# A hybrid attention and mixture-of-experts kernel: nine hidden chunks instead of six before the first expert weights, and a new order of the side steps

## The chip, the cores and the metric

The kernel runs on one core of a Trainium2 chip. The metric is the device time of one execution in microseconds (us). TensorE (PE in the profile) multiplies into eight PSUM banks, VectorE (DVE), ScalarE (ACT) and GpSimd (POOL) do the element work, and SyncE (SP) issues all DMA transfers. Each engine runs its own instructions strictly in the order of the program, and a wait on a semaphore holds up everything behind it on that engine.

## The reference

Four sequences ("rows") of 1024 tokens with 128 features each go through four residual blocks:

```python
x = x + attn_a(layernorm(x))   # no softmax: per-token 8x8 kv sums over heads, rms norms, gelu MLP
x = x + ffn(layernorm(x))      # 32 experts of width 64; the top 8 weigh, all 32 are computed
x = x + attn_b(layernorm(x))   # causal softmax attention, 16 heads, window of 64
x = x + ffn(layernorm(x))
# ffn: for each expert  acc += (u * silu(g)) @ dw.T * w_e[:, None]
```

## The kernel before, in words

**Chunks.** A row is two groups of 512 tokens, and each group goes through the ffn twice, so a row has four ffn stages `f` = 0 to 3 and the kernel 16 of them. A stage is 16 chunks; a chunk is two experts (128 hidden values) by 512 tokens. For each chunk PE makes the gate and the up product (`gate_up`, three matmuls each, since the operands are split into a high and a low part), ACT applies silu from PSUM into a buffer `work` (`silu`), DVE multiplies the up product in (`gated`), POOL multiplies the experts' combination weights in (`hidden`), and PE multiplies by the down weights (`down`, two instructions in the trace), which adds into one bank. In the stream `down` follows `gate_up` by three chunks. The gate and up banks hold three chunks, `work` holds six.

**Combination weights.** A stage's weights are made by the steps `route`, `r_sum`, `top`, `weigh`, `comb`, `cnorm` and `weighT`. The last one copies them into `combT` on ACT; SP sends that to DRAM (L649) and reads it back spread over the partitions in four quarters of four chunks, the first as eight transfers (L661), the others as two each (L666). The spread buffer holds two quarters; a later quarter waits until POOL is done with the one before in its place.

**Side steps.** Everything else (norms, the first attention, MLP, projections) is cut into named steps. `PLAN` is a table written out by hand or by a search: for each stage, which steps stand behind which chunk ("slot"). `own`, `ahead` and `back` say whether the step is of this row, the next or the one before. Each engine runs through the table and executes its own half of each step, so a step moved in the table moves on every engine that takes part. During the softmax attention, which has stages of its own (`attn`, three slots for each tile of 128 tokens), the same table is used. `x_stats` is the start of a norm on DVE and waits for the row's input transfer `x_buf<-x` (L631); `m_stats`, `m_rstd` (POOL), `m_apply` (ACT), `moe_turn` (PE), `z_hi` (ACT), `z_lo` (DVE) are the norm ahead of an ffn stage; `h_sq1` to `h_sum` are the rms norms of the first attention; `attend` (POOL), `kvsum`, `wterm`, `wred` (DVE) are its sums for one tile; `seq_turn`, `keys`, `queries`, `values` prepare the softmax attention.

**The lead.** Before the first stage no weights are there. `AHEAD` is the order of the steps until then. In it `early n` is PE's `gate_up` of chunk n and `lead n` is ACT's `silu` and DVE's `gated` of that chunk; `FIRST` says how many chunks stand there. `elu_first`, `qkv_first`, `qkv_next`, `expo` and `qscale` are the steps of the first attention on ACT and PE, `w_hi` and `w_lo` split the expert weights, `masks` are constants on POOL.

Of the kernel before, what the change touches and what calls it, by code (L numbers as in the profile page):

```python
# [80 lines left out]
def back(*steps):  # L81
# [3 lines left out]
FIRST = 6  # L85
# [15 lines left out]
        15: ahead(("qkv", 5)),
    },
    (0, "third"): {
        0: ahead(("wred", 3), ("h_sq1", 0), ("h_red1", 0), ("h_g2", 0), ("h_newton1", 0), ("qkv", 6), ("h_sq2", 0)),
        1: ahead(("h_red2", 0), ("qkv", 7), ("h_pow2", 0), ("h_newton2", 0)),
        3: own(("y_back", 0), ("s_stats", 0)) + ahead(("h_scale", 0), ("h_gain", 0), ("h_sum", 0)) +
            own(("s_rstd", 0)),
        4: ahead(("expo", 1), ("elu", 1)),
        5: ahead(("qscale", 1)),
        6: ahead(("attnT", 0), ("attend", 4), ("x_add", 0)),  # L110
        7: ahead(("mlp1", 0)),
        8: ahead(("attend", 5)) + own(("s_apply", 0)) + ahead(("mlp2", 0)),
        10: own(("bias", 0)) + ahead(("kvsum", 4)) + own(("seq_turn", 0)),
        11: ahead(("wterm", 4)) + own(("keys", 0)) + ahead(("m_stats", 0), ("m_rstd", 0)),
        12: own(("queries", 0)),
        14: ahead(("m_apply", 0)) + own(("values", 0)) + ahead(("kvsum", 5)),
        15: ahead(("moe_turn", 0), ("attend", 6)),
# [1559 lines left out]
```

## Time and profile before

| what | us |
|---|---|
| median of 3 runs | 970.69 |
| lowest and highest run | 967.74, 975.84 |
| the profiled execution's own time | 970.32 |
| its span from first to last instruction | 968.5 |

The times below are counted from the start of the span; 1.8 us of the execution lie outside it. The busy shares are means over stages that are bound by different things, so each stage is read for itself.

### The profile page before, as it was taken

How to read it: one execution, taken by the hardware profiler on the slowest of the kernel's cores; microseconds unless marked ns; L12 is line 12 of the kernel's file. 1: busy time of each engine (PE TensorE's matmuls, PEld its weight loads, DVE VectorE, ACT ScalarE, POOL GpSimd, SP SyncE). 2: the span in 40 equal slices, each digit the busy share in tenths (PEclk: the TensorE clock that was granted, in tenths of full speed). 3: DMA queues.
4: the chain of work that ended last, by engine and by line, in shares of the span. 5: the costliest groups of instructions: out<-in, count | busy, mean ns of one | idle time of the engine just before them, and what ended most of it. 6: DMA issues, size and time to landing. Idle time of an engine off the chain costs nothing.

```text
span 968.5 us, 16816 instructions
## 1 busy us (share of the span) xinstructions
PE 895.2 (92%) x5456; PEld 623.2 (64%) x5456; DVE 653.0 (67%) x1471; ACT 611.6 (63%) x1876; POOL 663.8 (69%) x617
## 2 busy tenths in 40 slices
PE   2467999898999999999999999999999999999998
PEld 1145666685667666687666666687666667667665
DVE  5898876897768748698648756798635348447522
ACT  4446676993665576795775585896556377486531
POOL 6786888675687759576669768666666545646654
PEclk8559999999899999999999999999999999999999
DMA  6006254016343626240433534340344530713352
GB/s 193 0 1 142 52 128 89 2 46 136 64 123 76 139 60 157 58 121 13 98 92 87 146 83 108 74 129 17 87 106 102 135 68 27 159 38 102 88 133 65
DMA packets 64903, 85.75 MB, mean 89 GB/s; under 512 B 5232, under 2 KB 30768, under 8 KB 64560
## 3 DMA queue, kind: packets, MB, share of 16 engines
q1 hardware_dynamic: 64816, 84.68, 36.4%
q8 instruction: 43, 0.70, 0.3%
q14 instruction: 44, 0.36, 0.1%
HBM read 79.39 MB, written 5.28 MB: 87 GB/s over the span
## 4 chain that ended last, share of the span: by engine, by line
PE 69%; DVE 10%; ACT 7%; POOL 5%; issue 4%; DMA 3%; SPq 1%; DVEq 0%; ACTq 0%; POOLq 0%
PE bank L1542 19%; PE bank L1519 11%; PE bank L1521 10%; PE bank L1520 10%; ACT probs L1081 4%; PE bank L1578 4%; PE bank L1563 3%; PE bank L1592 2%; POOL work L872 2%; DVE probsT L1346 2%; PE bank L1406 1%; DMA spread_w<-comb_dram 1%; DVE w_terms L1188 1%; PE bank L1556 1%; DMA x_buf<-x 1%
## 5 line engine op out<-in xcount | busy, mean ns | idle before, releaser
L872 POOL TENSOR_TENSOR work<-work,spread_w 128x512 f32<-128x512 f32 x256 | 333.8, 1318 | 171.0 <-DVE work L1304 151.7
L1304 DVE TENSOR_TENSOR work<-work,bank 128x512 f32<-128x512 f32 x256 | 172.1, 683 | 185.3 <-PE bank L1521 93.1
L1542 PE MATMUL bank<-work,down_w 128*128 128x512 f32 x512 | 262.7, 598 | 1.9 <-POOL work L872 1.9
L1056 ACT ACTIVATE work<-bank 128x512 f32<-128x512 f32 x256 | 150.3, 596 | 176.5 <-PE bank L1521 171.9
L1519 PE MATMUL bank<-z_hi,gate_hi 128*128 128x512 f32 x256 | 168.0, 656 | 4.9 <-ACT work L1056 2.7
L1081 ACT ACTIVATE probs<-bank,neg_max 128x96 f32<-128x96 f32 x512 | 166.3, 386 | 5.5 <-DVE neg_max L1332 3.9
L880 POOL TENSOR_TENSOR probs<-probs,prob_inv 128x768 f32<-128x768 f32 x64 | 95.1, 1486 | 59.9 <-DVE prob_inv L1340 59.6
L1081 ACT ACTIVATION_READ_ACCUMULATOR probs<-bank,neg_max 128x1 f32 x512 | 127.6, 252 | 0.0
L1542 PEld LDWEIGHTS bank<-work,down_w 128*128 128x128 f32 x512 | 95.3, 189 | 29.6 <-POOL work L872 5.6
L1519 PE MATMUL bank<-z_hi,up_hi 128*128 128x512 f32 x256 | 101.8, 397 | 3.1 <-DVE work L1304 3.1
L1521 PE MATMUL bank<-z_hi,gate_lo 128*128 128x512 f32 x256 | 102.0, 398 | 0.0
L1521 PE MATMUL bank<-z_hi,up_lo 128*128 128x512 f32 x256 | 101.5, 397 | 0.0
L1520 PE MATMUL bank<-z_lo,gate_hi 128*128 128x512 f32 x256 | 101.2, 395 | 0.0
L1520 PE MATMUL bank<-z_lo,up_hi 128*128 128x512 f32 x256 | 100.4, 392 | 0.0
L829 POOL TENSOR_TENSOR kv_terms<-elu,qkv 128x1024 f32<-128x1024 f32 x32 | 81.8, 2562 | 12.5 <-DVE elu L1153 7.2
L1346 DVE COPY probsT<-bank 96x512 f32<-96x512 f32 x128 | 80.2, 666 | 3.6 <-PE bank L1578 3.2
L1332 DVE TENSOR_REDUCE neg_max<-bank 128x4 f32<-128x384 f32 x128 | 64.8, 547 | 20.1 <-PE bank L1563 19.2
L1519 PEld LDWEIGHTS bank<-z_hi,gate_hi 128*128 128x128 f32 x256 | 49.0, 191 | 42.4 <-issue 31.0
L1578 PE MATMUL bank<-ident,probs 128*96 128x128 f32 x512 | 69.8, 278 | 6.8 <-DVE probsT L1346 6.0
L1520 PEld LDWEIGHTS bank<-z_lo,gate_hi 128*128 128x128 f32 x256 | 49.3, 193 | 33.7 <-issue 30.6
L1563 PE MATMUL bank<-keysT,qm 32*128 32x96 f32 x1024 | 69.2, 269 | 0.0
L1563 PEld LDWEIGHTS bank<-keysT,qm 32*128 32x128 f32 x1024 | 66.4, 188 | 0.0
(155 smaller groups left out, 1467.2 us busy)
## 6 DMA issues: line engine op xcount, KB each, us to landing
spread_w<-comb_dram SPq DMA_DIRECT2D x96, 512.0 KB, 6.7
spread_w<-comb_dram SPq DMA_DIRECT2D x128, 128.0 KB, 3.0
vals<-v_dram SPq DMA_DIRECT2D x16, 384.0 KB, 4.0
x_buf<-x SPq DMA_DIRECT2D x8, 256.0 KB, 4.3
v_dram<-v_tok SPq DMA_DIRECT2D x8, 256.0 KB, 6.8
out<-xs SPq DMA_DIRECT2D x8, 256.0 KB, 3.1
spread_w<-wg SPq DMA_DIRECT2D x1, 1024.0 KB, 7.1
spread_w<-wu SPq DMA_DIRECT2D x1, 1024.0 KB, 9.2
```

The costliest lines, as they stand in the source:

```text
L872: pool.tensor_tensor(work[:, n % WORK], work[:, n % WORK], spread_w[:, n // EACH % 2, s % EACH], ALU.mult).then_inc(hid_gated, 1)
L880: pool.tensor_tensor(pr, pr, prob_inv[:, i % 2, part].unsqueeze(2).broadcast_to([P, HALF_BLOCKS, KW]), ALU.mult).then_inc(probs_normed, 1)
L1056: act.activation(work[:, n % WORK], bank[GATE_BANKS[ring_of(row, f, s)]], ACT.Silu).then_inc(silu_ready, 1)
L1081: a = act.activation(probs[:, i % 2, m], bank[hg][:, b * KW:(b + 1) * KW], ACT.Exp, bias=neg_max[:, i % 2, m:m + 1], accum_out=prob_sum[:, ...
L1304: dve.tensor_tensor(work[:, n % WORK], work[:, n % WORK], bank[UP_BANKS[ring_of(row, f, s)]], ALU.mult).then_inc(gated_ready, 1)
L1346: dve.tensor_copy(probsT[:, b], bank[4 + b % 2][0:KW, :]).then_inc(probsT_copied, 1)
L1519: pe.matmul(dst, w_hi[:, cols], h, start=True, stop=False)
L1520: pe.matmul(dst, w_hi[:, cols], l, start=False, stop=False)
L1521: pe.matmul(dst, w_lo[:, cols], h, start=False, stop=True).then_inc(ready, 1)
L1542: pe.matmul(bank[Y_BANK], down_w[:, c], work[:, n % WORK], start=(c == 0), stop=(c == CH - 1)).then_inc(down_done, 1)
L1563: mm = pe.matmul(bank[hg][:, KW * b:KW * (b + 1)], qm[feats, i // T, NB * (i % T) + b].rearrange("p j q -> p (j q)"), keysT[feats, first:f ...
L1578: mm = pe.transpose(bank[4 + b % 2][0:KW, P * hg:P * (hg + 1)], probs[:, i % 2, hg * NB + b], ident[:])
```

## The change

`FIRST` becomes 9. Chunks 6 to 8 of the first stage have no room in `work`, so they go into `probs`, the buffer of the softmax probabilities, which is not in use yet; `work_of` says where a chunk lies, and `work_before` which chunk has to be through its `down` product before a buffer is written again. Both tables, `PLAN` and `AHEAD`, are replaced as a whole: the same steps in another order.

```diff
-FIRST = 6
+FIRST = 9
...
     (0, "first"): {
...
-        9: ahead(("x_stats", 1), ("x_rstd", 1)) + own(("m_apply", 1)),
-        10: own(("moe_turn", 1)) + ahead(("attend", 2), ("attend", 3)) + own(("z_hi", 1), ("z_lo", 1)),
+        9: own(("m_apply", 1)) + ahead(("kvsum", 1), ("wterm", 1)) + own(("moe_turn", 1), ("z_hi", 1)) +
+            ahead(("attend", 2)) + own(("z_lo", 1)) + ahead(("x_apply", 1)),
...
     (0, "attn"): {
...
-        25: ahead(("weighT", 0)),
+        19: ahead(("weighT", 0)),
...
     (1, "third"): {
-        0: ahead(("wterm", 3)),
...
+        1: own(("seq_turn", 0)) + ahead(("wterm", 3)) + own(("values", 0)),
...
+        def work_of(n):
+
+            if WORK <= n < FIRST:
+                return probs[:].rearrange("p r m k -> p r (m k)")[:, (n - WORK) // 3, GT * ((n - WORK) % 3):GT * ((n - WORK) % 3 + 1)]
+            return work[:, (n if n < WORK else n - FIRST) % WORK]
+
+        def work_before(n):
+            return n - (FIRST if n < FIRST + WORK else WORK) if n >= FIRST else -1
...
-                wait(act, down_done, n - WORK + 1)
-                act.activation(work[:, n % WORK], bank[GATE_BANKS[ring_of(row, f, s)]], ACT.Silu).then_inc(silu_ready, 1)
+                wait(act, down_done, work_before(n) + 1)
+                act.activation(work_of(n), bank[GATE_BANKS[ring_of(row, f, s)]], ACT.Silu).then_inc(silu_ready, 1)
...
-                pe.matmul(bank[Y_BANK], down_w[:, c], work[:, n % WORK], start=(c == 0),
+                pe.matmul(bank[Y_BANK], down_w[:, c], work_of(n), start=(c == 0),
```

Three places show what the tables do. The first is ACT at the end of the lead. `scratch<-attn` is `h_sq1`, `qkv<-bank` and the `elu<-bank` behind it are `qkv_next` 3, `elu<-elu 128x1024` is `expo`, `combT<-bank` is `weighT`, the writes of `work` are `lead`, and the two `elu<-elu 128x4x16x4` are `qscale`. Before:

```order
L984 ACTIVATE scratch<-attn 128x512
L964 ACTIVATE qkv<-bank 128x384
L965 ACTIVATE elu<-bank 128x256
L972 ACTIVATE elu<-elu 128x1024
L1025 ACTIVATE combT<-bank 32x512
L1056 ACT_TABLE_LOAD
L1056 ACTIVATE work<-bank 128x512 x2
```

Here is the same place on ACT after the change (eight lines further down in the file).

```order
L992 ACTIVATE scratch<-attn 128x512
L972 ACTIVATE qkv<-bank 128x384
L973 ACTIVATE elu<-bank 128x256
L980 ACTIVATE elu<-elu 128x1024
L1064 ACT_TABLE_LOAD
L1064 ACTIVATE work<-bank 128x512 x2
L986 ACTIVATE elu<-elu 128x4x16x4
L987 ACTIVATE elu<-elu,lam_coef 128x4x16x4
L1033 ACTIVATE combT<-bank 32x512
L1064 ACTIVATE work<-bank 128x512 x4
```

A table load, two `silu` and the two instructions of `qscale` now stand ahead of the copy that releases the weights.

The second place is POOL from the last side step of the lead through the first `hidden` products (`work<-work,spread_w`). `tok_rms` is the end of `h_pow2`, `x_buf<-x_buf,attn` is `x_add`, and `var_eps` to `shift` are a `rstd` step. Before:

```order
L872 TENSOR_TENSOR work<-work,spread_w 128x512 x3
L844 TENSOR_SCALAR tok_ms<-tok_ms 128x4
L845 TENSOR_TENSOR tok_rms<-tok_ms,minus_half 128x4
L872 TENSOR_TENSOR work<-work,spread_w 128x512 x2
L850 TENSOR_TENSOR x_buf<-x_buf,attn 128x512
L872 TENSOR_TENSOR work<-work,spread_w 128x512 x3
L815 TENSOR_SCALAR var_eps<-moments 128x4
```

The same stretch of POOL after the change:

```order
L852 TENSOR_SCALAR tok_ms<-tok_ms 128x4
L853 TENSOR_TENSOR tok_rms<-tok_ms,minus_half 128x4
L880 TENSOR_TENSOR work<-work,spread_w 128x512 x3
L858 TENSOR_TENSOR x_buf<-x_buf,attn 128x512
L880 TENSOR_TENSOR work<-work,spread_w 128x512 x3
L880 TENSOR_TENSOR probs<-probs,spread_w 128x512
L823 TENSOR_SCALAR var_eps<-moments 128x4
```

`x_add` moved from behind chunk 4 to behind chunk 2, `h_pow2` ahead of chunk 0, and `m_rstd` from behind chunk 7 to behind chunk 6.

The third place is DVE in the first ffn stage of row 1, `(1, "first")`: `w_terms` and `attn<-w_terms` are `wterm` 7 and `wred` 7, `xs<-x_buf,bank` is `proj`, `stats<-x_buf` is `x_stats` of row 2, and each `work<-work,bank` is `gated` of one chunk. Before:

```order
L1304 TENSOR_TENSOR work<-work,bank 128x512
L1188 TENSOR_TENSOR w_terms<-elu,kv 128x1024
L1194 TENSOR_REDUCE attn<-w_terms 128x128
L1139 BN_STATS stats<-x_buf 128x6 x4
L1142 BN_AGGR moments<-stats 128x2 x4
L1304 TENSOR_TENSOR work<-work,bank 128x512 x3
```

The same stage on DVE after the change:

```order
L1202 TENSOR_REDUCE attn<-w_terms 128x128
L1254 TENSOR_TENSOR xs<-x_buf,bank 128x512
L1312 TENSOR_TENSOR work<-work,bank 128x512 x2
L1266 TENSOR_TENSOR z_lo<-bank,z_hi 128x512
L1147 BN_STATS stats<-x_buf 128x6 x4
L1150 BN_AGGR moments<-stats 128x2 x4
L1207 TENSOR_REDUCE head_ms<-scratch 128x64
```

`x_stats` moved from behind chunk 3 to behind chunk 5, and `z_lo` stands ahead of it now.

## Rows read from the trace of the kernel before

**Rows 1.** The page, parts 1 and 2: busy time, and the granted clock in 40 slices.
```profile
PE 895.2 (92%) x5456; PEld 623.2 (64%) x5456; DVE 653.0 (67%) x1471; ACT 611.6 (63%) x1876; POOL 663.8 (69%) x617
...
PEclk8559999999899999999999999999999999999999
```

**Rows 2.** Busy time by stretch: length, then each engine, granted clock, DMA share, GB/s.
```profile
13.90:72.46 58.56, 28.05 (x66) 14.82 (x65) 54.13 (x95) 27.16 (x67) 45.85 (x38) 0.56 0.08 26
...
94.15:129.22 35.07, 33.19 (x133) 22.41 (x134) 27.88 (x66) 21.36 (x46) 28.69 (x25) 1.00 0.39 94
...
230.19:280.48 50.29, 46.74 (x170) 31.35 (x171) 34.12 (x71) 30.36 (x57) 33.22 (x28) 0.93 0.50 114
...
396.17:457.02 60.85, 57.83 (x728) 44.83 (x727) 48.60 (x106) 50.05 (x268) 40.15 (x40) 1.00 0.23 60
```

**Rows 3.** Timeline of ACT, end of the lead: start, length, what, idle time before.
```profile
72.49 0.63 ACT L984 ACTIVATE scratch<-attn 128x512 f32<-128x512 f32 x1 [1.45 <-DVE attn L1194]
...
73.81 1.06 ACT L972 ACTIVATE elu<-elu 128x1024 f32<-128x1024 f32 x1
75.95 0.59 ACT L1025 ACTIVATE combT<-bank 32x512 f32<-32x512 f32 x1 [1.09 <-PE bank L1461]
76.64 1.28 ACT L1056 ACT_TABLE_LOAD   x1
77.94 1.09 ACT L1056 ACTIVATE work<-bank 128x512 f32<-128x512 f32 x2
...
79.43 0.42 ACT L978 ACTIVATE elu<-elu 128x256 f32<-128x256 f32 x1
79.74 0.50 ACT L979 ACTIVATE elu<-elu,lam_coef 128x256 f32<-128x256 f32 x1
```

**Rows 4.** Timeline of SP and of POOL around the first quarters of weights.
```profile
76.56 0.35 SPq L649 DMA_DIRECT2D comb_dram<-combT  x1
...
92.81 1.29 POOL L872 TENSOR_TENSOR work<-work,spread_w 128x512 f32<-128x512 f32 x1 [4.53 <-DMA spread_w<-comb_dram]
...
99.14 1.15 POOL L815 TENSOR_SCALAR var_eps<-moments 128x4 f32<-128x4 f32 x1
...
101.97 2.50 POOL L872 TENSOR_TENSOR work<-work,spread_w 128x512 f32<-128x512 f32 x2
```

**Rows 5.** Timeline of PE behind the first weights.
```profile
94.15 1.12 PE L1542 MATMUL bank<-work,down_w 128*128 128x512 f32 x2 [0.35 <-POOL work L872]
95.11 1.05 PE L1440 MATMUL bank<-w_w,attnT 128*128 128x128 f32 x8
...
101.65 0.40 PE L1521 MATMUL bank<-z_hi,up_lo 128*128 128x512 f32 x1
101.89 1.02 PE L1542 MATMUL bank<-work,down_w 128*128 128x512 f32 x2
103.75 0.66 PE L1400 MATMUL bank<-ident,z 128*128 128x128 f32 x4 [0.83 <-ACT z L931]
```

**Rows 6.** Timelines of SP, DVE and PE, first ffn stage of row 1; a stretch of 3 us.
```profile
231.54 1.20 SPq L631 DMA_DIRECT2D x_buf<-x  x2
...
234.60 1.22 DVE L1194 TENSOR_REDUCE attn<-w_terms 128x128 f32<-128x1024 f32 x1
240.33 0.87 DVE L1139 BATCH_NORM_STATS2 stats<-x_buf 128x6 f32<-128x128 f32 x4 [4.50 <-DMA x_buf<-x]
...
242.24 0.50 PE L1519 MATMUL bank<-z_hi,up_hi 128*128 128x512 f32 x1 [3.07 <-DVE work L1304]
...
246.00:249.00 3.00, 3.00 (x11) 2.61 (x12) 1.52 (x3) 0.24 (x1) 2.67 (x6) 0.50 0.00 0
```

**Rows 7.** Timeline of DVE in the lead: the same operation twice.
```profile
49.04 3.26 DVE L1188 TENSOR_TENSOR w_terms<-elu,kv 128x1024 f32<-128x1024 f32 x1
...
56.90 1.22 DVE L1188 TENSOR_TENSOR w_terms<-elu,kv 128x1024 f32<-128x1024 f32 x1
```

**Rows 8.** Who waited for whom, from 125 us on: total, times, longest.
```profile
PE bank L1480 <- DVEq L1249: 0.9, 1, 0.9
```

More of the change, by code:

```diff
@@ L111 @@
[L111 to L117, printed above, removed]
+        0: ahead(("qkv", 6)),
+        1: ahead(("qkv", 7)),
@@ L173 @@
[L173 to L181 removed]
+        0: ahead(("wterm", 2), ("wred", 2), ("kvsum", 3)) + own(("weighT", 1)),
@@ new lines @@
+        6: own(("s_apply", 1)) + ahead(("attend", 6), ("moe_turn", 0), ("z_hi", 0)),
+        7: ahead(("z_lo", 0), ("route", 0), ("r_sum", 0), ("top", 0)),
+        8: ahead(("weigh", 0), ("comb", 0), ("kvsum", 5)) + own(("seq_turn", 1)),
+        9: ahead(("wterm", 5), ("wred", 5), ("kvsum", 6)) + own(("keys", 1)),
+        11: ahead(("attend", 7)) + own(("queries", 1), ("bias", 1)) + ahead(("wterm", 6), ("wred", 6)),
+        13: ahead(("kvsum", 7)) + own(("values", 1)) + ahead(("wterm", 7), ("cnorm", 0)),
@@ new lines @@
+        6: ahead(("x_apply", 0)),
+        7: back(("route", 2), ("r_sum", 2)) + own(("h_gain", 1)),
+        8: back(("top", 2)),
+        9: back(("weigh", 2)) + ahead(("x_turn", 0)),
+        10: ahead(("qkv", 0)) + back(("comb", 2)),
+        11: own(("h_sum", 1), ("attnT", 1)) + back(("cnorm", 2)) + ahead(("qkv", 1)) + own(("x_add", 1)),
+        12: back(("weighT", 2)),
+        13: own(("mlp1", 1)) + ahead(("qkv", 2)),
+        14: own(("mlp2", 1)),
+        15: own(("m_stats", 1), ("m_rstd", 1)) + ahead(("qkv", 3)),
@@ new lines @@
+    (2, "fourth"): {
+        0: own(("queries", 0)),
+        3: ahead(("mlp2", 0), ("m_stats", 0), ("m_rstd", 0)),
+        4: own(("y_back", 1), ("s_stats", 1), ("s_rstd", 1)),
+        5: ahead(("wterm", 4), ("wred", 4), ("kvsum", 5), ("m_apply", 0)),
+        6: ahead(("moe_turn", 0), ("z_hi", 0), ("z_lo", 0)) + own(("s_apply", 1)) + ahead(("wterm", 5)),
+        8: ahead(("route", 0)),
+        9: ahead(("r_sum", 0), ("top", 0), ("wred", 5), ("attend", 6), ("weigh", 0), ("comb", 0)),
+        10: own(("values", 0)) + ahead(("cnorm", 0), ("kvsum", 6)),
+        11: own(("seq_turn", 1)),
+        12: ahead(("wterm", 6)) + own(("keys", 1)),
+        13: own(("queries", 1)),
+        14: own(("values", 1)) + ahead(("wred", 6)),
+    },
@@ L291 @@
-    (3, "second"): {
-        0: own(("mlp1", 1)),
-        1: own(("mlp2", 1), ("m_stats", 1)),
-        2: own(("m_rstd", 1)),
-        5: own(("m_apply", 1)),
-        6: own(("moe_turn", 1), ("z_hi", 1), ("z_lo", 1)),
-        7: own(("route", 1), ("r_sum", 1), ("top", 1)),
-        9: own(("weigh", 1), ("comb", 1), ("cnorm", 1), ("y_back", 0), ("s_stats", 0), ("s_rstd", 0)),
-        10: back(("m_stats", 3), ("m_rstd", 3)),
-        12: own(("s_apply", 0), ("weighT", 1)),
-        14: own(("bias", 0)) + back(("m_apply", 3)),
-        15: own(("seq_turn", 0)),
-    },
```

414 lines of the change are left out of this document (200 added, 214 removed).

## The prediction

> **What bounds the kernel now.** The page comes first: PE is busy for 92% of the span, the next engine for 69% [rows 1], so the most that any new order can win is PE's idle time, 73 us, plus what the lower clock costs. The slices of the granted clock say where that lies: 8, 5, 5, 5 at the start, an 8 behind 190 us, a 9 behind 240, and 9s after that [rows 1]. The table by stretch then parts the kernel in three.
>
> The lead is DVE's. From 13.90 us to 72.46 DVE is busy for 54.13 us of 58.56 and PE for 28.05, at a mean clock of 0.56 [rows 2]. Time that PE loses there counts only through the moment at which the first weights come. That chain is read in the timelines: DVE's last sum ends at 72.46, ACT makes `h_sq1`, `qkv_next` 3 and `expo`, copies the weights out at 75.95 and SP sends them at 76.56 [rows 3, 4]. The second quarter lands in time for `hidden` of chunk 4 at 92.81, for which POOL waited 4.53 us [rows 4], and PE's `down` of it starts at 94.15 [rows 5]: 17.6 us after the send. From there to the first `down` of the next stage at 129.22 PE is busy for 33.19 of 35.07 us [rows 2].
>
> The first ffn stage of row 1 has a wait that can be named. DVE finishes the last first-attention sum at 235.82 and stands for 4.50 us, until 240.33, in `x_stats` of row 2: its two transfers `x_buf<-x` were issued at 231.54 only [rows 6]. `gated` of the next chunks is queued behind it on DVE, so PE stands for 3.07 us, and a stretch behind it runs at clock 0.50 though PE is never idle in it [rows 6]. 0.50 is the 1.2 GHz level, 1.00 is 2.4 GHz. The stage takes 50.29 us with 46.74 of PE and a mean clock of 0.93 [rows 2].
>
> Elsewhere PE is close to full: a softmax stage of 60.85 us has 57.83 of PE [rows 2], and the longest wait of the same kind as a bunched norm behind 125 us is 0.9 us [rows 8]. A new order there can give little and may take some.
>
> **The change, part by part.**
>
> *Ahead of the first weights.* On DVE the same steps stand before the last sum, with `x_stats` of the second group moved into an idle place before 13.90 us. It holds four `BN_STATS`, 0.87 us [rows 6], and its closing aggregate; I estimate 1.25 for both, so the last sum ends at 71.2. Bounds: if the rest of DVE's idle time went too, 58.56 - 54.13 = 4.4 us [rows 2], it would end at 66.8. If one `w_terms` met a POOL instruction more than before, 3.26 - 1.22 = 2.0 us [rows 7], it would end at 74.5 with none of the gain. I take 71.2, since the order on DVE hardly changes.
>
> Behind that sum ACT now has more to do. Before, from 72.49 to the copy's end at 76.54, ACT made three steps and waited 1.09 us for PE [rows 3]. Now it is `h_sq1` and `qkv_next` 3 (73.81 - 72.49 = 1.32), `expo` 1.06, the table load with the gap around it (77.94 - 76.54 = 1.40), two `silu` in 1.09, `qscale` in two instructions (79.43 to 80.24, 0.81) and the copy in 0.59 [rows 3]. Together 6.3 us, since `h_sq1` is the first of them and waits for the last sum: from 71.2 to 77.5, where the copy ends, one microsecond later than before.
>
> So `hidden` of chunk 4 comes 16.25 us after the send, as it did, at about 93.8, and `down` of it at 95.1. PE then has less to do before the next stage: one group of gate and up products stands earlier (six starts 0.24 apart, 1.40 us) and so does `mlp2` (under 1.05) [rows 5], 31.0 us in place of 33.19. But `m_rstd` stands behind `hidden` of 4, 5 and 6 on POOL. These take 1.25 each (2.50 for two), `m_rstd` 2.83 (99.14 to 101.97), and `m_apply` with PE's start another 1.78 (101.97 to 103.75) [rows 4, 5]. So `moe_turn` can start at 93.8 + 3.7 + 2.8 + 1.8 = 102.1, while PE has three `down` of 0.96 and one group of 1.40 until then and is through at 99.4. It idles for 2.7 us. The stage's end: 95.1 + 31.0 + 2.7 + 0.3 of the idle time that the stage had besides, and half a microsecond for `probs` as a new buffer, is 129.6, against 129.22: **+0.4**.
>
> The nine chunks let PE finish its early products sooner and wait longer before the weights come. Where PE waited like that the clock fell to 0.50 (the 3.00 us stretch in [rows 6]). One such spell, taken as twice that stretch and a little, 6.8 us at half rate, costs 3.4 us. It may come or not, so I take half, **+1.7**. Bounds of the lead in all: -3 with an early last sum and no spell, +7 with a late one and a spell. Sum: **+2.1**.
>
> *The Trainium skill on this.* ACT's switch of tables shows 1.28 us of load, and 1.40 from the end of the copy to the first `silu` [rows 3]. The Trainium skill, page "ScalarE: Activation LUTs", section "What ACT_TABLE_LOAD costs", adds a drain of 1.38 us to a load of 1.28. By it the copy would come 1.3 us later still, and the whole 968.2; the trace shows no room for such a drain.
>
> *The wait of row 1's first stage.* `weighT` of row 1 moves from slot 25 to slot 19 of the softmax stage of row 0, two tiles earlier. A stage of eight tiles takes 60.85 us where I have it as a row [rows 2], so two tiles are some 15 us, in the quicker stages nearer 11. SP sends the input of row 2 behind the quarters of these weights, so it is issued earlier by about as much, at 220 to 222. On top of that `x_stats` moves two slots later, about 4.5 us. A transfer issued at 231.54 was there at 240.33; one issued ten microseconds earlier is there at 230, well ahead of a reader at 240. The wait goes. What it cost: 50.29 - 46.74 = 3.55 us of PE idle and 0.07 x 50.29 = 3.5 us of clock [rows 2], together 7.0. The four `BN_STATS` still stand ahead of a `gated`, and `z_lo` now with them, so something of the idle time stays: **-6.5**, between -7 and -4 (the 4 is the 4.50 us wait without its clock).
>
> *Side steps put together.* In several places steps that had slots between them now share one: `seq_turn` and `values` of the softmax attention, `z_lo` with `route`, and `weigh`, `comb` and `cnorm` in slot 12 of the second stages. Each engine does the same work, but PE must wait for a copy on another engine inside a slot. The nearest row is PE waiting 0.9 us for DVE, the longest of its pair behind 125 us [rows 8]. I price one such wait net of what the other moves give back: **+1.0**, from 0 to +5 (five places at 0.9).
>
> *Softmax stages.* They have 3.02 us of PE idle in 60.85 [rows 2]; the moves put fewer norm steps into some and more into others. **0**, within 3 us either way, what one stage has.
>
> **How the numbers follow.** The profiled execution took 970.32 us, 1.8 of them outside the span, and the median of three is 970.69; I start from the first. 970.32 + 2.1 - 6.5 + 1.0 + 0 = 966.9, so **967** us, 0.4% faster. A measurement of this kernel can hardly tell less than 1%, 9.7 us, from no change.
>
> **Rivals.**
>
> *Faster by over 1%.* The rest of DVE's 4.4 us of idle time in the lead goes as well, and the last sum ends at 66.8. The copy ends 6.3 us later, at 73.1, 3.4 us earlier than before. The stage behind it gives another 0.6 (the terms above: +0.4 with a copy 1.0 later), the early products keep the clock at 1.00, and nothing is lost by the side steps: 970.3 - 3.4 - 0.6 - 6.5 = 959.8. For it speaks that DVE alone bounds the lead; against it, that ACT has two `silu`, a table load and `qscale` more ahead of the copy, and that little moves on DVE there. Chance 0.25.
>
> *Slower than before.* In the lead the same `w_terms` takes 1.22 us in one place and 3.26 in another [rows 7]; I take it that a POOL instruction beside it is the cause. If the new order lets three more of them meet one before the last sum, it comes 6.1 us later, and the clock's 3.4 us are due in full: 970.3 + 6.1 + 0.4 + 3.4 - 6.5 + 1.0 = 974.7. It decides from 1.7 us of such clashes on (6.5 - 1.0 - 3.4 - 0.4). Against it: nearly all sums of the lead stand where they stood. Chance 0.12. The Trainium skill, page "SBUF — State Buffer", section "SBUF: two separate sides", has the port pair that these two engines share as an exclusive lock, held for a whole instruction; by that rule each meeting costs up to the other's length, and the two lengths in [rows 7] agree with it.
>
> *The gain doesn't come, or comes back.* If the transfer still lands late, or the new slot makes DVE late for `gated` in the same way, 6.5 shrinks to 1: 972. For it: four steps stand behind `x_stats` in the slot now. Against it: the ten microseconds of lead. Chance 0.13.
>
> The forecast itself has 0.50. The range is **955 to 977**: the lower end is the faster rival with 3 us more from the softmax stages and something from the side steps, the upper the slower rival with half the side steps' bound on top. Faster by over 1%, below 961: 0.18 of the faster rival's 0.25, and 0.12 from the forecast with two of its terms at their lower bounds, **0.30**. Slower by over 1%, beyond 980: the slower rival with the softmax and side steps' upper bounds besides, **0.07**. Within 1%: **0.63**.
>
> **What would show it.** In the profile after, DVE should have no wait on `x_buf<-x` in row 1's first stage, and that stage should take about 44 us at a clock near 1.00. SP's first `comb_dram<-combT` should stand near 77.5 us, the first `down` of the second stage near 129.6 to 131, with a PE wait of some 2.7 us ahead of `moe_turn`. PE waits inside the slots named should not pass 1 us. The prediction is wrong if the first send comes at 72 or 82, if the clock falls in stages where it held, or if the softmax stages change by more than 3 us each.

## The result, and the profile after

The changed kernel takes 975.53 us (median of 20 runs, 973.28 to 986.20), the kernel before 970.60 (20 runs). The ratio is 1.0066 with a 95% interval of 1.0046 to 1.0087, so 4.5 to 8.4 us slower. Two of the profiled executions below, that of the spread steps and that of nine chunks in the kernel before, were disturbed ones with a low clock over long stretches, and the ratios leave such executions out. The forecast was 967: the time lies in its range of 955 to 977, but on the other side of no change. The interval is 0.2% to either side, so a change well under the 1% that the prediction called hard to tell can be told here.

The two profiled spans, 968.5 and 975.6 us, differ by 7.1, the medians by 4.9: the spans are those of one pair of executions. Since every ffn stage begins with the `down` of its chunk 0 on PE, the span can be cut there in both traces, and the difference falls on a few stretches:

| stretch, by the first `down` of its stage | before | after | difference | forecast |
|---|---|---|---|---|
| start to row 0's second stage | 129.22 | 129.06 | -0.2 | +2.1 |
| that stage and the softmax stage of row 0 | 100.97 | 102.45 | +1.5 | 0 |
| `(1, "first")` | 50.29 | 43.87 | **-6.4** | -6.5 |
| `(1, "second")` to the end of row 1's softmax stage | 176.54 | 178.11 | +1.6 | +1.0 for all side steps |
| `(2, "first")` to `(2, "third")` | 126.91 | 130.47 | **+3.6** | in the above |
| `(2, "fourth")` and the softmax stage of row 2 | 94.47 | 97.17 | **+2.7** | 0 |
| `(3, "first")` to the end of row 3's softmax stage | 215.56 | 214.83 | -0.7 | 0 |
| `(4, "second")` | 38.78 | 43.80 | **+5.0** | not in the sum |
| `(4, "fourth")` to the end | 35.76 | 35.84 | +0.1 | 0 |

The differences of `(1, "second")` to `(2, "third")` come back within 0.2 us in all other profiles that share these tables. Those of the lead and of row 0's softmax stage don't: profiles with the lead of the kernel before begin the second stage at 128.3 to 130.0, and those with the changed lead and nine chunks at 128.1 to 130.4, so the -0.2 is no difference.

The gain is there and has the size that was forecast. It is lost again in places that the sum priced too low or left out. The page of the profile after, parts 1 and 2, answers to [rows 1]: PE has the same busy time, only the span is longer.

```profile
PE 894.6 (92%) x5456; PEld 621.8 (64%) x5456; DVE 656.3 (67%) x1471; ACT 610.8 (63%) x1876; POOL 665.9 (68%) x617
...
PEclk8568999999999999999999999999999999999999
```

Timeline of the changed kernel at the end of the lead, answering to [rows 3 to 5]: start, length, what, idle time before and who ended it.

```profile
71.72 1.19 DVE L1202 TENSOR_REDUCE attn<-w_terms 128x128 f32<-128x1024 f32 x1
...
74.25 1.06 ACT L980 ACTIVATE elu<-elu 128x1024 f32<-128x1024 f32 x1
75.33 1.28 ACT L1064 ACT_TABLE_LOAD   x1
76.62 1.09 ACT L1064 ACTIVATE work<-bank 128x512 f32<-128x512 f32 x2
...
78.30 0.57 ACT L1033 ACTIVATE combT<-bank 32x512 f32<-32x512 f32 x1
...
78.90 0.35 SPq L657 DMA_DIRECT2D comb_dram<-combT  x1
...
102.60 0.66 PE L1408 MATMUL bank<-ident,z 128*128 128x128 f32 x4 [1.44 <-ACT z L939]
```

In the same kernel the clock was low ahead of the send (length, PE busy, granted clock, DMA share, GB/s):

```profile
75.00:78.00 3.00, 2.93 (x8) 0.50 0.02 5
```

The last sum ends at 72.91 and not at 71.2, the weights are sent 2.3 us later than before, and still the next stage begins no later. PE waits 1.44 us ahead of `moe_turn` where 2.7 were forecast. That PE has less left to do behind the weights, with nine chunks made ahead, is the likely reason; no run shows it apart from the clock.

The first ffn stage of row 1 in the changed kernel, answering to [rows 6]: SP's last issue of weights ahead of the input, its issue of the input, DVE around `x_stats`, and the stage as a stretch (length, PE busy, granted clock, DMA share, GB/s).

```profile
222.26 1.26 SPq L674 DMA_DIRECT2D spread_w<-comb_dram  x2
223.56 13.80 SPq L639 DMA_DIRECT2D x_buf<-x  x2
...
239.13 0.69 DVE L1266 TENSOR_TENSOR z_lo<-bank,z_hi 128x512 fp32r<-128x512 f32 x1 [0.65 <-ACT z_hi L1015]
239.74 0.86 DVE L1147 BATCH_NORM_STATS2 stats<-x_buf 128x6 f32<-128x128 f32 x4
...
231.51:275.38 43.87, 43.87 (x178) 1.00 0.39 94
```

The first of the two transfers is issued 8 us earlier than before, DVE does not wait, PE is never idle and the clock holds. This is the forecast's main step, as it was put. Its size depends on the execution of the kernel before that it is set against: in five profiles of kernels that have both steps of this stage as before it takes 50.3 to 51.9 us, and the one used here is the shortest. The gain is 6.4 to 8.0 us, and that it meets -6.5 so closely is in part luck.

Now `(4, "second")`, the last but one stage. First the kernel before: SP's store of the attention's output, DVE's `proj`, which overwrites what is stored, and the stage.

```profile
883.01 0.60 SPq L691 DMA_DIRECT2D out<-xs  x1
...
896.12 0.69 DVE L1246 TENSOR_TENSOR xs<-x_buf,bank 128x512 f32<-128x512 f32 x1 [1.82 <-PE bank L1495]
...
893.96:932.74 38.78, 38.78 (x152) 1.00 0.38 89
```

The same in the changed kernel, with SP's issue of weights ahead of the store, the start of PE's `moe_turn` and a stretch behind it:

```profile
892.90 1.26 SPq L674 DMA_DIRECT2D spread_w<-comb_dram  x2
894.20 0.60 SPq L699 DMA_DIRECT2D out<-xs  x1
...
902.01 0.69 DVE L1254 TENSOR_TENSOR xs<-x_buf,bank 128x512 f32<-128x512 f32 x1 [5.72 <-DMA out<-xs]
...
908.00 0.66 PE L1408 MATMUL bank<-ident,z 128*128 128x128 f32 x4 [3.27 <-ACT z L939]
...
895.96:939.76 43.80, 40.52 (x152) 0.96 0.43 104
...
909.00:912.00 3.00, 3.00 (x8) 0.56 0.02 5
```

The store is issued 11.2 us later, DVE waits 5.72 us for it, the norm behind `proj` is late, PE idles 3.27 us ahead of `moe_turn`, and then the clock is at its lower level for a while.

### The profile page after: what moved, and what is told of

Same layout as the page of the kernel before. It is cut to its first block, busy times and chain, and to the rows that moved or that the text cites. A ratio compares the mean times of both kernels' runs of the same rounds, so it can differ in the third digit from the quotient of the medians.

```text
span 975.6 us, 16815 instructions
## 1 busy us (share of the span) xinstructions
PE 894.6 (92%) x5456; PEld 621.8 (64%) x5456; DVE 656.3 (67%) x1471; ACT 610.8 (63%) x1876; POOL 665.9 (68%) x617
## 4 chain that ended last, share of the span: by engine, by line
PE 66%; DVE 10%; ACT 9%; POOL 8%; issue 4%; DMA 1%; SPq 1%; DVEq 0%; POOLq 0%; ACTq 0%
PE bank L1550 19%; PE bank L1527 10%; PE bank L1529 10%; PE bank L1528 10%; ACT probs L1089 5%; PE bank L1571 3%; POOL work L880 3%; PE bank L1586 2%; POOL probs L888 2%; PE bank L1408 1%; DVE probsT L1354 1%; PE bank L1600 1%; PE bank L1414 1%; PE bank L1564 1%; POOL rstd L824 1%
## 5 line engine op out<-in xcount | busy, mean ns | idle before, releaser
L1312 DVE TENSOR_TENSOR work<-work,bank 128x512 f32<-128x512 f32 x253 | 169.2, 683 | 189.9 <-PE bank L1529 94.3
L1550 PE MATMUL bank<-work,down_w 128*128 128x512 f32 x506 | 259.9, 598 | 3.7 <-POOL work L880 3.5
L1064 ACT ACTIVATE work<-bank 128x512 f32<-128x512 f32 x253 | 148.3, 596 | 175.2 <-PE bank L1529 172.3
L1089 ACT ACTIVATION_READ_ACCUMULATOR probs<-bank,neg_max 128x1 f32 x512 | 125.2, 247 | 0.0
L1586 PEld LDWEIGHTS bank<-ident,probs 128*96 128x96 f32 x512 | 53.7, 127 | 22.4 <-issue 12.5
```

The costliest lines, as they stand in the source:

```text
L1064: act.activation(work_of(n), bank[GATE_BANKS[ring_of(row, f, s)]], ACT.Silu).then_inc(silu_ready, 1)
L1089: a = act.activation(probs[:, i % 2, m], bank[hg][:, b * KW:(b + 1) * KW], ACT.Exp, bias=neg_max[:, i % 2, m:m + 1], accum_out=prob_sum[:, ...
L1312: dve.tensor_tensor(work_of(n), work_of(n), bank[UP_BANKS[ring_of(row, f, s)]], ALU.mult).then_inc(gated_ready, 1)
L1550: pe.matmul(bank[Y_BANK], down_w[:, c], work_of(n), start=(c == 0), stop=(c == CH - 1)).then_inc(down_done, 1)
L1586: mm = pe.transpose(bank[4 + b % 2][0:KW, P * hg:P * (hg + 1)], probs[:, i % 2, hg * NB + b], ident[:])
```

## Experiments

### The late store, in both directions

In the softmax half `(3, "attn_hi")` the change moved `weighT` of row 3's third stage from slot 5 to slot 10. On SP the store `out<-xs` stands behind the transfers of these weights. The one number was put back in the changed kernel:

```diff
     (3, "attn_hi"): {
         3: back(("y_back", 3)),
-        10: own(("weighT", 2)),
+        5: own(("weighT", 2)),
```

> The changed kernel with one number put back: the weights of the next to last stage are released in slot 5 of the last softmax half, not in slot 10. Theory: SP's store of xs stands behind the transfers of these weights, so it is issued 11 us too late and DVE's proj waits 5.7 us for it; with slot 5 the wait goes, the stage shortens by 5.0 us (3.3 of PE idle time, 1.7 of the clock) and the whole comes to about 970.5. Rival: the store is late because its step moved from slot 2 to 3, or DVE waits for something else then: 974 to 976, no change.

Measured: 971.96 us against 968.82 for the kernel before, ratio 1.0037 (1.0017 to 1.0057). Stage and store in this run:

```profile
885.00 0.60 SPq L699 DMA_DIRECT2D out<-xs  x1
...
896.14:934.79 38.65, 38.65 (x152) 1.00 0.37 90
```

And the other way, with the same two numbers, in the kernel before:

> The kernel before with the same number changed the other way: weights of the next to last stage released in slot 10, not 5. Theory: 5.0 us slower than before, 975.6, with a DVE wait of some 5 us for the store ahead of proj. Rival (the wait needs the other moves of the change as well): within 1 us of before.

Measured: 975.58 us, ratio 1.0062 (1.0032 to 1.0093).

```profile
897.26 0.60 SPq L691 DMA_DIRECT2D out<-xs  x1
...
904.72 0.69 DVE L1246 TENSOR_TENSOR xs<-x_buf,bank 128x512 f32<-128x512 f32 x1 [4.86 <-DMA out<-xs]
...
899.52:942.63 43.11, 40.66 (x153) 0.96 0.42 102
```

The stage goes from 43.80 to 38.65 with slot 5 and from 38.78 to 43.11 with slot 10, and the wait goes and comes with it. The mechanism holds. Its price is less even: the run with slot 5 came down from a ratio of 1.0066 to 1.0037, some 3 us of the 5.0 expected, and the run with slot 10 went up by 6; both are known to about 3 us only. In two other profiles with slot 10, of the steps set apart and of the spread steps below, the clock holds in this stage and it takes 41.1 and 41.3 us. So PE's idle time is worth some 2.5 us there without the low clock, and 4.3 to 5.2 with it. The rival, that `y_back` had moved by a slot, falls: it stayed in slot 3 in the first run and in 2 in the second.

### Where the gain comes from

The kernel before with the weights of row 1 two tiles earlier, and nothing else:

```diff
     (0, "attn"): {
+        19: ahead(("weighT", 0)),
         22: own(("proj", 0)),
         23: own(("m_stats", 2), ("m_rstd", 2)),
-        25: ahead(("weighT", 0)),
```

> The kernel before with the second weights released in slot 19 of the softmax stage of row 0, not 25; x_stats stays in slot 3. Theory: the input transfer is issued some 11 us earlier, DVE's wait of 4.50 us goes and with it PE's idle time and the low clock, 6.4 us in all: 964.2. Rival: the slot of x_stats is what counts, and most of the wait stays: 968 to 970.6.

Measured: 962.51 us, ratio **0.9941** (0.9919 to 0.9963). DVE runs `x_stats` at 237.39 with no wait, and the stage is even 1.0 us shorter than in the changed kernel:

```profile
231.62:274.47 42.85, 42.85 (x171) 1.00 0.38 97
```

The other half of the pair alone, in the kernel before:

```diff
     (1, "first"): {
-        3: own(("wterm", 7)) + back(("moe_turn", 2)) + own(("wred", 7)) + ahead(("x_stats", 0)),
+        3: own(("wterm", 7)) + back(("moe_turn", 2)) + own(("wred", 7)),
+        5: ahead(("x_stats", 0)),
```

> The kernel before with x_stats of the next row two slots later (5, not 3) in the first stage of row 1; the weights stay in slot 25. Theory: the two slots are worth 4.5 us, as long as the wait was, so most of it goes as well and either part of the pair is enough: first stage of row 1 43 to 45 us, the whole 963 to 966. Rival: the transfer is late by more than the wait shows (it shares the queues with weights), 1 to 3 us of wait stay and the clock falls all the same: 967 to 970.

Measured: 966.41 us, ratio 0.9973 (0.9945 to 1.0000), between the two. In its profile DVE still waits, since it comes two `gated` later but the transfer does not come sooner:

```profile
243.31 0.87 DVE L1140 BATCH_NORM_STATS2 stats<-x_buf 128x6 f32<-128x128 f32 x4 [3.59 <-DMA x_buf<-x]
...
232.68:281.75 49.07, 46.62 (x171) 0.93 0.48 116
```

So the earlier issue is what takes the wait away. The later reader alone is worth 1.2 us by this pair of profiles and 3.3 by the medians, with an interval from nothing to 5.3. My expectation that either part is enough fell.

### Two sums in one slot of a softmax tile

In the softmax stage of row 2 the change put `wterm` 7 and `wred` 7 in slot 23, where the last tile drains. The end of that stage before, POOL's normalisation of the probabilities and PE's last turn of them, and the stage:

```profile
666.61 1.47 POOL L880 TENSOR_TENSOR probs<-probs,prob_inv 128x768 f32<-128x768 f32 x1 [1.03 <-DVE prob_inv L1340]
...
672.21 1.15 PE L1578 MATMUL bank<-ident,probs 128*96 128x128 f32 x8 [1.54 <-DVE probsT L1346]
...
583.93:678.40 94.47, 90.12 (x860) 1.00 0.32 78
```

The same in the changed kernel:

```profile
665.93 3.55 POOL L888 TENSOR_TENSOR probs<-probs,prob_inv 128x768 f32<-128x768 f32 x1 [1.03 <-DVE prob_inv L1348]
...
666.93 1.21 DVE L1196 TENSOR_TENSOR w_terms<-elu,kv 128x1024 f32<-128x1024 f32 x1
668.17 1.22 DVE L1202 TENSOR_REDUCE attn<-w_terms 128x128 f32<-128x1024 f32 x1
670.80 0.69 DVE L1361 TENSOR_TENSOR mix_all<-bank,head_mask 128x512 f32<-128x512 f32 x1 [1.40 <-POOL mixT L896]
...
672.83 1.17 PE L1586 MATMUL bank<-ident,probs 128*96 128x128 f32 x8 [2.22 <-DVE probsT L1354]
...
583.96:681.13 97.17, 91.95 (x874) 0.98 0.30 74
...
674.00:677.00 3.00, 3.00 (x37) 0.50 0.02 5
```

POOL's normalisation ends at 669.48 instead of 668.08, so its next product `mixT` comes later, DVE waits 1.40 us for that ahead of `mix_all`, and DVE's copy `probsT`, for which PE waits, stands behind `mix_all`. PE's wait grows from 1.54 to 2.22 us, and this time the clock is at 0.50 behind it. The kernel before was given that order:

```diff
     (2, "attn"): {
         0: ahead(("weighT", 0), ("kvsum", 7)) + own(("bias", 1)),
-        2: ahead(("wterm", 7)) + back(("y_back", 3)),
-        6: ahead(("wred", 7)),
-        10: ahead(("h_sq1", 1)),
-        11: ahead(("h_g2", 1)),
-        14: ahead(("h_red1", 1)),
-        23: ahead(("h_newton1", 1)),
+        2: back(("y_back", 3)),
+        23: ahead(("wterm", 7), ("wred", 7)),
+        25: ahead(("h_sq1", 1), ("h_red1", 1)),
     (3, "first"): {
+        0: own(("h_newton1", 1), ("h_g2", 1)),
```

> The kernel before with the changed kernel's order of the late steps in the softmax stage of row 2: wterm 7 and wred 7 in slot 23, h_sq1 and h_red1 in 25, h_newton1 and h_g2 at the start of the ffn stage behind. Theory: the spell at the stage's end grows from 1.5 to 2.2 us and the clock falls behind it: the stage 2.7 us longer, the whole 971.5 to 973. Rival: within 1 us of before, and the 2.7 us come from something else of the change in that stage.

Measured: 973.69 us, ratio 1.0043 (1.0016 to 1.0069). The stage takes 2.7 us more, as in the changed kernel, with the same POOL row:

```profile
664.02 3.54 POOL L878 TENSOR_TENSOR probs<-probs,prob_inv 128x768 f32<-128x768 f32 x1 [1.02 <-DVE prob_inv L1338]
...
582.34:679.54 97.20, 92.14 (x859) 0.96 0.30 75
```

So these steps in this place cost the 2.7 us. Other profiles agree: with the steps as in the kernel before the stage takes 94.3 to 94.5 us in seven of them, and with the steps in slot 23 it takes 97.15 to 97.20 in four. A fifth, of six chunks below, has 99.72, with the clock low for longer. To get them back in the changed kernel was tried three times. First another tile:

```diff
     (2, "attn"): {
-        23: ahead(("wterm", 7), ("wred", 7)),
+        20: ahead(("wterm", 7), ("wred", 7)),
```

> The changed kernel with wterm 7 and wred 7 in slot 20 of the softmax stage of row 2, not 23. Theory: in slot 23 they hold POOL's normalisation of the probabilities at 3.55 us in place of 1.47, PE idles for 2.22 us at the stage's end and the clock falls to 0.50 for 4 us behind it; in slot 20 PE has other work, and 2.7 us come back: 972.8. Rival: the stage's end is short of work whatever DVE does, and the same clash costs as much in slot 20: 975.5.

Measured: ratio 1.0126 (1.0086 to 1.0167), and the stage is 2.4 us longer still:

```profile
670.77 2.38 DVE L1196 TENSOR_TENSOR w_terms<-elu,kv 128x1024 f32<-128x1024 f32 x1
...
592.97:692.58 99.61, 93.24 (x873) 0.97 0.29 73
```

`w_terms` takes 2.38 us beside POOL there, DVE's maxima of the next scores stand behind both sums, PE waits 2.94 us in that tile and the clock falls there instead. The theory that a place with other PE work hides them falls. Then the steps were spread over the stage:

```diff
     (2, "attn"): {
-        1: own(("bias", 0)),
+        1: own(("bias", 0)) + ahead(("attend", 7)),
+        3: ahead(("kvsum", 7)),
+        5: ahead(("wterm", 7)),
-        15: ahead(("attend", 7)),
-        18: ahead(("kvsum", 7)),
-        23: ahead(("wterm", 7), ("wred", 7)),
-        25: ahead(("h_sq1", 1), ("h_red1", 1)),
+        10: ahead(("wred", 7)),
+        14: ahead(("h_sq1", 1)),
+        17: ahead(("h_red1", 1)),
```

> The changed kernel with the seven steps of the softmax stage of row 2 spread as in the kernel before: attend 7 in slot 1, kvsum 7 in 3, wterm 7 in 5, wred 7 in 10, h_sq1 in 14, h_red1 in 17. Theory: a softmax tile has room for one DVE step of about 1.2 us in its slot, not for two in a row (2.4 us), whatever tile it is; moving both to slot 20 did not help, parting them does. The idle spell of 2.2 us at the stage's end and the low clock behind it go: the stage 2.7 us shorter than in the changed kernel, 94.5 us, the whole about 972.8. Rival: it is the end of the stage that wants the time, or w_terms costs wherever it stands: less than 1 us.

Measured: ratio 1.0138 (1.0072 to 1.0204). In the profiled execution the clock was at 0.50 from some 637 to 685 us:

```profile
651.00:675.00 24.00, 24.00 (x218) 0.50 0.07 18
```

Its stage of 116.75 us says nothing of the steps, so this run is inconclusive for the spreading; it only shows no gain. Then out of the softmax stage into the ffn stage behind it:

```diff
     (2, "attn"): {
-        23: ahead(("wterm", 7), ("wred", 7)),
-        25: ahead(("h_sq1", 1), ("h_red1", 1)),
     (3, "first"): {
-        0: back(("proj", 0), ("m_stats", 2), ("m_rstd", 2)),
-        2: own(("h_newton1", 1), ("h_g2", 1)) + back(("proj", 1)),
+        0: back(("proj", 0), ("m_stats", 2), ("m_rstd", 2)) + own(("wterm", 7)),
+        1: own(("wred", 7), ("h_sq1", 1)),
+        2: own(("h_red1", 1), ("h_newton1", 1), ("h_g2", 1)) + back(("proj", 1)),
```

> The changed kernel with wterm 7, wred 7, h_sq1 and h_red1 taken out of the softmax stage of row 2 into slots 0 to 2 of the ffn stage behind it. The runs so far say that the two sums on DVE cost time wherever in the softmax stage they stand together. Theory: without them PE's idle spell of 2.2 us at the stage's end is below 1.6 us, the clock stays at 1.00 behind it, the stage takes 94 to 94.5 us, and the ffn stage takes them at no cost: 972.8. Rival: the ffn stage pays for them (DVE late with gated): 974.5 to 976.

Measured: 977.95 us, ratio 1.0105 (1.0060 to 1.0150). The ffn stage pays: PE waits 1.78 us ahead of `moe_turn`, as DVE comes to `proj` late, and the stage goes from 40.05 to 43.71.

```profile
684.71:728.42 43.71, 40.88 (x159) 1.00 0.29 70
```

The rival holds. The softmax stage itself took 99.49 us in this run, with the clock low in its middle; in the run with three repairs below, where the clock held, the same steps took 93.96.

### Steps that share a slot

PE's waits in four of these places in the changed kernel (`values` behind `seq_turn`, `route` behind `z_lo`, `qkv` behind `attnT` and behind `mlp1`):

```profile
311.98 1.16 PE L1495 MATMUL bank<-qkv_b_w,seqT 128*128 128x128 f32 x8 [0.69 <-ACT seqT L930]
...
373.53 0.30 PE L1459 MATMUL bank<-router_hl,z_hi 128*128 128x64 f32 x1 [0.90 <-DVE z_lo L1266]
...
478.02 0.91 PE L1414 MATMUL bank<-qkv_a_w,zT 128*128 128x384 f32 x2 [0.69 <-ACT attnT L930]
...
485.38 0.91 PE L1414 MATMUL bank<-qkv_a_w,zT 128*128 128x384 f32 x2 [0.69 <-ACT attnT L1011]
```

The kernel before got the same four pairs:

```diff
     (1, "second"): {
-        15: ahead(("kvsum", 3)) + own(("seq_turn", 0)) + ahead(("x_stats", 1)),
+        15: ahead(("kvsum", 3)) + ahead(("x_stats", 1)),
     (1, "third"): {
-        1: ... + own(("values", 0)) + ...
+        1: ... + own(("seq_turn", 0), ("values", 0)) + ...
     (1, "fourth"): {
-        6: ahead(("moe_turn", 0), ("z_hi", 0), ("z_lo", 0)),
-        7: ahead(("route", 0), ...
+        6: ahead(("moe_turn", 0), ("z_hi", 0)),
+        7: ahead(("z_lo", 0), ("route", 0), ...
     (2, "first"): {
-        10: back(("weigh", 2)) + own(("attnT", 1)),
-        11: ahead(("qkv", 1)) + back(("comb", 2), ("cnorm", 2)),
-        12: ahead(("qkv", 2)),
-        14: own(("mlp1", 1)),
+        10: back(("weigh", 2)),
+        11: own(("attnT", 1)) + back(("comb", 2), ("cnorm", 2)) + ahead(("qkv", 1)),
+        14: own(("mlp1", 1)) + ahead(("qkv", 2)),
```

> The kernel before with the four pairs of the changed kernel put in one slot each: qkv 1 behind attnT, qkv 2 behind mlp1, seq_turn ahead of values, z_lo ahead of route. Theory: each costs PE 0.7 to 0.9 us of idle time, 3 us in all: the four stages that hold them together 3 us longer, the whole 972.5 to 973.5. Rival (PE would have waited elsewhere anyway): the sum of these stages within 1 us of before.

Measured: 974.02 us against 968.88, ratio 1.0067 (1.0040 to 1.0093). By the first `down` of each stage, the stretch from `(1, "second")` to the end of row 1's softmax stage takes 177.65 us (+1.1) and that from `(2, "first")` to `(2, "third")` 130.51 (+3.6), together 4.7, where the changed kernel has +1.6 and +3.6, together 5.1 before rounding. One of the waits:

```profile
480.82 0.91 PE L1405 MATMUL bank<-qkv_a_w,zT 128*128 128x384 f32 x2 [1.12 <-ACT attnT L921]
```

The pairs cost by themselves, and more than the waits in front of them: of the 3.6 us in `(2, "first")` to `(2, "third")`, 1.1 are PE's busy time (127.91 us, and 127.89 in the changed kernel, against 126.78) and the rest is idle time. Why the busy time grows is not shown. Stage by stage the two kernels agree less than in these sums: `(1, "second")` takes 2.6 us more than before in the changed kernel and 0.9 more in this one, so that the pairs are the whole of the changed kernel's 5.1 us is not shown either. Setting them apart in the changed kernel (`x_turn`, `qkv` 0 and 1 one slot earlier, `qkv` 2 and 3 later, `s_apply` and `seq_turn` so that `seq_turn` stands one slot ahead of `values`, `z_lo` in the slot of `z_hi`) is another matter, shown here for two of them:

```diff
     (1, "fourth"): {
-        6: own(("s_apply", 1)) + ahead(("attend", 6), ("moe_turn", 0), ("z_hi", 0)),
-        7: ahead(("z_lo", 0), ("route", 0), ("r_sum", 0), ("top", 0)),
+        6: own(("s_apply", 1)) + ahead(("attend", 6), ("moe_turn", 0), ("z_hi", 0), ("z_lo", 0)),
+        7: ahead(("route", 0), ("r_sum", 0), ("top", 0)),
     (2, "first"): {
-        13: own(("mlp1", 1)) + ahead(("qkv", 2)),
-        15: own(("m_stats", 1), ("m_rstd", 1)) + ahead(("qkv", 3)),
+        13: own(("mlp1", 1)),
+        15: own(("m_stats", 1), ("m_rstd", 1)) + ahead(("qkv", 2)),
```

> The changed kernel with steps that shared a slot set apart again: qkv 1 no longer behind attnT, qkv 2 no longer behind mlp1, seq_turn one slot ahead of values, z_lo one slot ahead of route. Theory: in each of these places PE waits 0.7 to 0.9 us for the engine that empties the one side bank; four places, so the first to fourth stages of row 1 and the first of row 2 lose together 2.5 to 3 us of idle time: 972.7. Rival: the idle time only moves to the next step that is late, less than 1 us.

Measured: 977.28 us, ratio 1.0072 (1.0043 to 1.0100), no gain. The four waits are gone, and others are there: `seq_turn` now comes too soon behind `s_apply`, and the first `down` of the next stage waits.

```profile
306.84 0.66 PE L1409 MATMUL bank<-ident,z 128*128 128x128 f32 x4 [1.47 <-ACT z L940]
...
319.15 1.13 PE L1551 MATMUL bank<-work,down_w 128*128 128x512 f32 x2 [1.35 <-POOL work L881]
```

Only `z_lo` paid (the stretch with `(1, "fourth")` is 1.1 us shorter). Here the rival holds: these pairs could not be parted in this way without new waits for their neighbours.

### Nine chunks

The changed kernel with six chunks ahead:

```diff
-FIRST = 9
+FIRST = 6
 AHEAD = (
...
-        ("h_g2", 1), ("early", 4), ("early", 5), ("early", 6), ("h_sq2", 1)) + ahead(("attend", 1)) +
-        own(("h_red2", 1), ("early", 7), ("h_pow2", 1), ("h_newton2", 1)) + ahead(("kvsum", 0)) + own(("lead", 6),
-        ("lead", 7), ("early", 8), ("h_scale", 1), ("h_gain", 1), ("lead", 8), ("h_sum", 1))
+        ("h_g2", 1), ("early", 4), ("early", 5), ("h_sq2", 1)) + ahead(("attend", 1)) +
+        own(("h_red2", 1), ("h_pow2", 1), ("h_newton2", 1)) + ahead(("kvsum", 0)) + own(
+        ("h_scale", 1), ("h_gain", 1), ("h_sum", 1))
```

> The changed kernel with six chunks ahead of the first weights, not nine; all tables else as changed. Theory: PE idles for some 4.7 us between 88 and 103 us for POOL and for side steps, and the three groups of 1.40 us that are taken back fit into that but for one: first stage 0 to 1.5 us later, 975.5 to 977. Rival (the three chunks pay in full): 4.2 us later, 979.7.

Measured: ratio 1.0108 (1.0064 to 1.0153), and the second stage begins at 132.85, 3.8 us later than with nine. That is near the rival's 4.2, but the clock was at 0.50 for some 7 us while PE worked off its first `down` products, and by the price that the prediction puts on such a spell this alone is 3.4. So what the three groups of products cost is not shown, and the interval of this ratio overlaps with that of the changed kernel.

```profile
87.00:90.00 3.00, 3.00 (x4) 0.50 1.02 231
```

The kernel before with nine, its own tables else (`work_of` and `work_before` as in the change):

```diff
-FIRST = 6
+FIRST = 9
 AHEAD = (
...
-        own(("lead", 3), ("lead", 4), ("lead", 5))
+        own(("lead", 3), ("lead", 4), ("lead", 5), ("early", 6), ("early", 7), ("early", 8),
+        ("lead", 6), ("lead", 7), ("lead", 8))
```

> The kernel before with nine chunks ahead of the first weights, three of them in the probabilities' buffer, and its own tables else. Theory: only the group of chunk 8 leaves the stretch behind the first weights, so the next stage begins at most 1.4 us earlier: 969.2 to 970.6. Rival: ACT and DVE do three more chunks ahead of the second group's norms, which come late: slower by 1 to 3 us.

Measured: ratio 1.0016 (0.9987 to 1.0045), no difference to be told. By its profile the second stage begins 2.6 us later, again with a low clock, 0.50 from 96 to 99 us.

And the kernel before from `(1, "first")` on, with all that stands ahead of it as in the changed kernel but for four steps:

```diff
     (0, "attn"): {
-        15: ahead(("kvsum", 6), ("weigh", 0)),
+        15: ahead(("weigh", 0)),
...
-        26: ahead(("wterm", 6)),
+        23: own(("m_stats", 2), ("m_rstd", 2)),
```

> The kernel before from row 1's first stage on, with everything ahead of it (the lead with nine chunks, the two ffn stages and the softmax stage of row 0, second weights in slot 19) as in the changed kernel. Theory: the lead is worth nothing here (stage starts within 0.2 us), the softmax stage of row 0 costs 1.5 us, row 1's first stage gains 6.4 to 7.4: 963.5 to 966, no better than the kernel before with slot 19 alone (962.5). Rival: nine chunks gain 1 to 4 us by a clock that holds: 959 to 961.

Measured: 964.31 us, ratio 0.9959 (0.9935 to 0.9983). It has the gain of slot 19 and nothing beyond: the second stage begins at 128.30, within what the lead of the kernel before gives by itself, and `(1, "first")` takes 42.90. The new lead with its nine chunks buys nothing over the old one with six.

### Three repairs at once

The changed kernel with `weighT` in slot 5, the sums out of the softmax stage and `z_lo` a slot earlier, each as above:

> The changed kernel with three repairs at once: the weights of the next to last stage in slot 5 (5.0 us by its own run's trace), the two sums of row 2 out of the softmax stage (2.7 us), z_lo of row 1 one slot ahead of route (1.1 us). Theory: the three add up, 975.5 - 8.8 = 966.7, below the kernel before. Rival: they do not add up, as each idle spell that goes lets another come late: 969 to 972.

Measured: 972.55 us against 969.67, ratio 1.0027 (1.0003 to 1.0051). They don't add up to the 8.8 us expected: the ratio is hardly below that of slot 5 alone, 1.0037. The stage of row 2 gains 3.2 us against the changed kernel (93.96) and the ffn stage behind it pays 3.7 (43.73); the other two repairs are in full in the trace. The best of all runs is the kernel before with one line moved, 0.9941.

## Why the prediction was wrong

**The wait of row 1's first stage** was read rightly, its cause (SP's issue behind the weights), its price (-6.5 forecast, -6.4 by this pair of profiles, up to -8.0 by others) and what removes it. The single move that the argument rests on gives the gain alone.

**The step that failed first is one that the sum left out.** The prediction followed one `weighT` past SP's queue and did not follow the other that the tables move, from slot 5 to 10 in `(3, "attn_hi")`. It is the same mechanism with the sign turned round: a transfer stands on SP behind a stage's weights, these are released later, and DVE waits for it. The sum has no term for this move, so it stood at nothing without a reason; the two runs that change the number alone show 4.3 to 5.2 us by their stage, with the low clock that followed.

**"Side steps put together", +1.0 with bounds of 0 and 5, measured 5.1.** The price of one place was right (0.7 to 0.9 in each of the four). What failed is "one such wait net of what the other moves give back": what came back did not pay for the others. Two of the four places, `qkv` behind `attnT` and behind `mlp1`, were not among those named, and they lie in the stretch with the larger loss, +3.6. The same pairs in the kernel before cost 4.7.

**"Softmax stages: 0, within 3 us"** holds its bound for each in this pair, but the +2.7 of row 2 has the mechanism that the prediction reads into [rows 7], for the lead only: a sum on DVE and POOL in each other's way. It served as a rival in the lead, where it did not come (the longest `w_terms` there is now 2.05 us), and not in the softmax stage, where POOL and DVE alternate in every tile. What goes with it is the low clock behind PE's wait, worth some 1.8 us more of PE's busy time in that stage (91.95 - 90.12).

**The lead**, +2.1, came out at -0.2. The copy ended at 78.87, later than 77.5, since the last sum came 1.7 later than thought: `x_stats` did move ahead, to 10.63 us, but DVE's busy time from 13.90 to the last sum fell by 0.3 us (54.13 to 53.84) and not by 1.25, and its idle time there grew by 0.7. The spell of low clock that was priced at half of 3.4 us fell ahead of the weights, and the stage behind did not come later for it. This error worked against the wrong sign and not for it. The drain of 1.38 us that the Trainium skill, page "ScalarE: Activation LUTs", section "What ACT_TABLE_LOAD costs", adds to a table load is not to be seen here either: `expo` ends at 75.31, the load runs from 75.33 to 76.61 and `silu` begins at 76.62.

**The rivals.** The slower one, 974.7, came within a microsecond of the median by luck, since its mechanism did not happen. The third, that the input's wait stays, did not happen either. None of the three named a new wait late in the program. One of the prediction's own signs of being wrong did come: the clock fell in two stages where it had held, `(4, "second")` and the softmax stage of row 2.

The stretches cover the whole span, so their sum must be the difference of the spans: -0.2 + 1.5 - 6.4 + 5.1 + 2.7 - 0.7 + 5.0 + 0.1 = 7.1. What the experiments add is that the four large ones can be made one at a time in the kernel before. By their ratios these four edits come to some -6, +6, +4 and +6.5 us, together 11 where the changed kernel's own ratio gives 6; each is uncertain by 2 to 3 us, so this neither closes nor contradicts the sum. The +1.5 around row 0's softmax stage is not explained by a step. The same steps there took 99.59 us in one experiment built on the kernel before and 104.92 in another, with nothing between them but the clock:

```profile
128.32:227.91 99.59, 95.14 (x888) 1.00 0.23 55
```

```profile
128.85:233.77 104.92, 100.78 (x887) 0.93 0.22 54
```

What stays open is whether the steps of row 2, spread over the softmax stage, would be free in the changed kernel where the clock holds, how much of the 5.1 is each pair's own, and what makes the clock fall in one execution and hold in another.

## What to carry to other kernels

When a table moves many steps, list every move of a step that issues a transfer, at both ends of the program, and for each name what stands behind it on the queue and who waits for that; one such move made this change's gain, and another of the same kind gave 3 to 6 us of it back. Price steps that are put together by count and not net, until a row shows what comes back. And when a change of many parts has one part with a clear mechanism, run that part alone: here it is the fastest of the versions that were run.

## What was not expected of the hardware

A POOL instruction grows beside DVE's work. The normalisation takes 1.47 us alone and 3.54 or 3.55 with `w_terms` and its reduction beside it, though it began 1.0 us ahead of `w_terms`. The Trainium skill, page "SBUF — State Buffer", section "SBUF: two separate sides", has the instruction that starts first keep the shared ports for its whole length, so that the other one waits. Here the one that starts first is the one that grows, and `w_terms` keeps its usual 1.21 us; the measurement decides, with the reservation that spans on POOL are rough.

Once down to 1.2 GHz in a softmax stage, the clock can stay there although PE is never idle: 24.00 us of 24.00 at 0.50 in the run with the spread steps. In the ffn stages of these runs it came back within the stage, after 3 to 10 us, but for the last one, which ended first.

A store of one group has a median of 3.0 us from issue to landing in the changed kernel, and the one behind the weights took 7.8:

```profile
DMA to landing us min/median/max: 2.3/3.0/7.8
```
